# Second tile's h loads on ScalarE's queue, weight staging re-spaced, first units reordered

## What is computed

```python
# layer 0: MLP whose last 128 outputs come from an expert picked by an index
h = gelu(einsum('bnd,hd->bnh', x, fc1_w) + fc1_b)              # hidden 2048
y = concat([einsum('bnh,sh->bns', h, fc2_w) + fc2_b,           # 384 outputs
            einsum('bnh,bph->bnp', h, experts_w[indices]) + experts_b[indices][:, None, :]], -1)
x = x + y
# layer 1: a linear layer picked by an index
x = x + einsum('bnh,boh->bno', x, weight[subject_id]) + bias[subject_id][:, None, :]
# layer 2: causal averages over time, gates, a normalised output
ctx = causal_ema(x, tau_ctx)
wg = sigmoid(einsum('btc,ec->bte', concat([x, ctx], -1), Wg) + bg)
# ... four gated traces, their blend "temporal" ...
gate = sigmoid(einsum('btc,ec->bte', temporal, Wtemp) + btemp)
soma = gelu(einsum('btc,ec->bte', x, Wsoma) + bsoma)
x = x + layernorm(einsum('btc,ec->bte', soma * gate, Wout)) * gamma + beta
# layer 3: a linear layer picked by an index
x = x + einsum('bnh,boh->bno', x, weight[ids]) + bias[ids][:, None, :]
```

## Time and profile before

| | before |
|---|---|
| median of 2 runs | 1416.73 us (1415.06 to 1418.4) |
| profiled execution | 1426.79 us, span 1425.1 us |
| PE busy | 1342.4 us, 94% of the span, 5725 matmuls |
| VectorE (DVE) busy | 1059.9 us, 74% |
| ScalarE (ACT) busy | 673.9 us, 47% |
| mean granted TensorE clock | 0.974 |
| DMA | 196.57 MB, mean 138 GB/s |

### The profile page before, as it was taken

One profiled execution on the slowest core, in us unless ns is written; L12 is line 12 of the kernel. 1 busy time (PEld: TensorE's weight loads), 2 busy tenths in 40 slices (PEclk: granted clock), 3 DMA queues, 4 the chain that ended last, 5 costly groups with the idle time before them and its releaser, 6 DMA issues.

```text
span 1425.1 us, 16400 instructions
## 1 busy us (share of the span) xinstructions
PE 1342.4 (94%) x5725; PEld 1090.7 (77%) x5725; DVE 1059.9 (74%) x1643; ACT 673.9 (47%) x1237; POOL 102.3 (7%) x135
## 2 busy tenths in 40 slices
PE   8889897989998999899999998999999999999998
PEld 6667685767786878787788787787888888888887
...
GB/s 259 77 93 200 196 152 81 130 184 169 197 137 137 111 206 204 187 133 134 141 228 236 208 157 175 178 185 51 104 45 163 52 97 54 153 71 54 99 8 67
DMA packets 102123, 196.57 MB, mean 138 GB/s; under 512 B 9705, under 2 KB 28137, under 8 KB 98969
## 3 DMA queue, kind: packets, MB, share of 16 engines
...
...
## 4 chain that ended last, share of the span: by engine, by line
PE 68%; DVE 16%; DMA 6%; ACT 5%; issue 4%; SPq 0%; DVEq 0%; POOL 0%; ACTq 0%; POOLq 0%
PE bank L1413 23%; PE bank L1414 22%; PE bank L1415 22%; DMA hb_in<-hb_dram 3%; DVE drive L2079 2%; DVE x_hl L1844 2%; DVE w_hl L1844 1%; DVE h_hl L1844 1%; DVE drive L2066 1%; DVE temporal L2094 1%; DMA stage<-in_wg 1%; ACT h_hl L983 1%; ACT bank L979 1%; DVE hb_out L1938 1%; DVE t_lo L1844 1%
## 5 line engine op out<-in xcount | busy, mean ns | idle before, releaser
L1413 PE MATMUL bank<-t_hi,sp_hl 128*128 128x512 f32 x448 | 186.6, 416 | 56.4 <-ACT p_sb L963 33.9
L1413 PE MATMUL bank<-h_hl,w_hl 128*128 128x512 f32 x512 | 203.4, 397 | 20.4 <-DVE w_hl L1844 20.2
L1415 PE MATMUL bank<-h_hl,w_hl 128*128 128x512 f32 x512 | 202.1, 395 | 0.0
L1414 PE MATMUL bank<-h_hl,w_hl 128*128 128x512 f32 x512 | 201.8, 394 | 0.0
L1414 PE MATMUL bank<-t_lo,sp_hl 128*128 128x512 f32 x448 | 182.7, 408 | 0.0
L1415 PE MATMUL bank<-t_hi,sp_hl 128*128 128x512 f32 x448 | 182.1, 406 | 0.0
L1413 PEld LDWEIGHTS bank<-t_hi,sp_hl 128*128 128x128 f32 x448 | 89.2, 199 | 86.1 <-ACT p_sb L963 39.4
L1413 PEld LDWEIGHTS bank<-h_hl,w_hl 128*128 128x128 f32 x512 | 97.9, 191 | 45.2 <-DVE h_hl L1844 24.8
L1415 PEld LDWEIGHTS bank<-h_hl,w_hl 128*128 128x128 f32 x512 | 97.6, 191 | 20.9
L1414 PEld LDWEIGHTS bank<-h_hl,w_hl 128*128 128x128 f32 x512 | 97.9, 191 | 20.2
L1415 PEld LDWEIGHTS bank<-t_hi,sp_hl 128*128 128x128 f32 x448 | 88.9, 199 | 19.7
...
## 6 DMA issues: line engine op xcount, KB each, us to landing
...
hb_dram<-hb_out SPq DMA_DIRECT2D x64, 256.0 KB, 3.7
hb_in<-hb_dram SPq DMA_DIRECT2D x64, 256.0 KB, 3.4
...
stage<-in_l_w SPq DMA_DIRECT2D x32, 256.0 KB, 3.4
...
```

The lines of the kernel that those rows point to most:

```text
L1413: eng.matmul(ps, w_hi, x_hi, start=first, stop=False, skip_group_check=resumed)
L1414: eng.matmul(ps, w_hi, x_lo, start=False, stop=False, skip_group_check=resumed)
L1415: return eng.matmul(ps, w_lo, x_hi, start=False, stop=final, skip_group_check=resumed)
```

## The change

The change has four parts. (1) `load_hb` moves from SP's list to ScalarE's: block 0's load stands ahead of the second tile's first split, block j + 1's at the head of block j's work. On SP the second tile holds only the staging and the expert weights' loads; in the last pair the loads of x, gate weights and soma weights, which stood between the h loads, follow each other. C12's store, and C12's Gelu on ScalarE, move behind P1's copy of the next unit; C12's addition on VectorE moves ahead of C21's low part. (2) Staging: two tables now say in which unit or block the parts are staged (pair 0 at j = 2, 6, 9, 12, pairs 1 and 2 at 3, 7, 11; unit 0 of pairs 1 to 3 now has one), TE parts all come before the WG parts, and of two parts in a unit the first one is split in mid-unit, the other at the end. (3) The first units of pair 0 run P6 before P5 (but for k = 0), and ScalarE's and VectorE's lists for them are in another order. (4) The loads of x's parts T3/B22 stand ahead of the reads of the indices, and seven of the eight reads come later.

```diff
-        FIRST_ORDER = ("P5", "P6", "P4", "P7", "P3")
+        FIRST_ORDER = [("P5", "P6", "P4", "P7", "P3")] + 3 * [("P6", "P5", "P4", "P7", "P3")]
...
-        PARKED = [("N1", 0)] + [("SO", c) for c in range(KC)] + [("TE", c) for c in range(2)]
-        PARKED += [("WG", c) for c in range(2 * KC)] + [("TE", c) for c in range(2, KC)]
+        PARKED = [("N1", 0)] + [("SO", c) for c in range(KC)] + [("TE", c) for c in range(KC)]
+        PARKED += [("WG", c) for c in range(2 * KC)]
...
+        parked_units = ((4, 5, 6, 7, K8 + 2, K8 + 6, K8 + 9, K8 + 12),
+                        (0, 1, 2, 4, 5, 7, K8 + 3, K8 + 7, K8 + 11),
+                        (0, 1, 2, 3, 4, 5, 6, 7, K8 + 3, K8 + 7, K8 + 11),
+                        (0, 1, 1, 2, 3, 4, 5, 6, 7))
+        l1_units = ((4, 5, 6, 7), (2, 3, 5, 6), (2, 3, 4, 5), (2, 3, 4, 5))
...
             load_w2(0)
+            load_part_b(0, 0)
+            load_part_b(0, 1)
             on.wait_ge(s_idx, 32)
-            expert = [nc.sync.value_load(idx[0:1, b:b + 1], min_val=0, max_val=EXPERTS - 1) for b in range(B)]
-            subject = [nc.sync.value_load(idx[0:1, B + b:B + b + 1], min_val=0, max_val=SUBJECTS - 1)
-                       for b in range(B)]
+            expert = [nc.sync.value_load(idx[0:1, 0:1], min_val=0, max_val=EXPERTS - 1)]
...
             for p in range(PAIRS):
                 for k in range(K8):
+                    if k:
+                        store_hb(p, k - 1, 0)
...
-                    store_hb(p, k, 0)
-                load_hb(p, 0)
+                if p < PAIRS - 1:
+                    load_part_b(p + 1, 1)
+                store_hb(p, K8 - 1, 0)
                 pass_staged(p, K8 - 1)
-                if p == PAIRS - 1:
-                    break
-                load_part_b(p + 1, 1)
-                for j in range(1, HC):
-                    load_hb(p, j)
+                for j in range(HC if p < PAIRS - 1 else 0):
                     if j in (10, 13):
+                        on.wait_ge(s_fc2, 2 * HC * p + HC + j - 3)
                         load_exp(p + 1, int(j == 13))
-                    if j >= 3:
-                        pass_staged(p, K8 + j - 3)
-                for j in range(HC - 3, HC):
                     pass_staged(p, K8 + j)
 
-            for j in range(1, HC):
-                load_hb(PAIRS - 1, j)
-                if j == 2:
-                    load_xt(0)
-                if j in (3, 5, 7):
-                    load_wg((j - 1) // 2)
...
+            load_xt(0)
+            load_wg(1)
+            load_wg(2)
+            load_wg(3)
+            load_wsoma(2)
+            load_wsoma(3)
+            store_x2(LAST - 1)
+            load_wsoma(0)
+            load_wsoma(1)
```

On ScalarE, in a unit:

```diff
                 p1_of(p, k)
+                if k:
+                    h_of_c12(p, k - 1)
...
                 h_of_c22(p, k)
-                for n in ahead[6:7]:
-                    product_hi(n)
+                staged_hi(p, k, slice(0, -1))
...
-                h_of_c12(p, k)
...
-                staged_hi(p, k)
+                staged_hi(p, k, slice(-1, None))
```

On ScalarE, behind a pair's units and in its second tile:

```diff
+                h_of_c12(p, K8 - 1)
+                load_hb(p, 0)
                 w2_hi(2 * HC * p + HC - 1)
                 for j in range(HC):
+                    if j + 1 < HC:
+                        load_hb(p, j + 1)
                     hb_hi(v)
```

On VectorE, in a unit:

```diff
                     product_lo(n)
+                staged_lo(p, k, slice(0, -1))
                 if p and k == 0:
-                    x1_of(t, 0)
-                    x1_of(t, 1)
+                    for m in range(KC):
+                        x1_of(t, m)
+                c12_of(p, k)
                 for n in ahead[6:7]:
                     product_lo(n)
...
-                h_lo_c21(p, k)
-                if p and k == 0:
                     x1_lo(t, 0)
                     x1_lo(t, 1)
-                c12_of(p, k)
+                h_lo_c21(p, k)
...
-                staged_lo(p, k)
+                staged_lo(p, k, slice(-1, None))
```

More of the change, by code:

```diff
@@ L1218, in _, with staged_hi @@
                 h_of_c21(0, k)
[L1219 to L1222 removed]
+            def staged_hi(p, u, at=slice(None)):
+                for n in staged_in[p, u][at]:
                     kind, a = staging[n]
@@ L1256, in unit @@
                     x1_hi(t, 1)
+                for n in ahead[6:7]:
+                    product_hi(n)
                 h_of_c21(p, k)
```

90 lines of the change are left out of this document (39 added, 51 removed).

## The result

The changed kernel takes 1355.78 us (median of two, 1355.22 to 1356.33) against 1416.73, a ratio of 0.957, 95% interval 0.9518 to 0.9621: 61 us faster. The profiled execution spans 1354.6 us where that of before spans 1425.1, 70.5 us less. The kernel before varies: beside the later experiments it took 1415 to 1435 us, and its profiled execution, 1426.8, is longer than the two timed here. The changed kernel's two times agree within 1 us.

A forecast was written before the change was run, and what follows sets the result against it. First 880 us bound by 116 us of PE waiting and half clock, the rest by PE. Stage gains summed to 83.0 us, off the profiled 1426.8 giving 1343.8, stated as 1340 because of slow stores; range 1322 to 1368.

The forecast's parts named there:

- The forecast case: Whole kernel: the stage gains come as summed, about 1340 us, own range 1322 to 1358; chance 0.70.
- sum of 83.0: First 880 us: gains of all nine stages added, 83.0 us, taken off the profiled 1426.8 to give 1343.8.
- the two stalls for P6: Unit 1 of pairs 2 and 3: new stalls of about 5 and 4 us, released by P1's copy.
- the last stall of about 6 us: Near the end of the last second tile: one stall of about 6 us, from a late h load, stays.
- (1 - clock) x us: First 880 us: clock loss reckoned per stage as missing clock share times stage time, 38 us in all.
- the 37.0: Pair 1's first tile, 214 to 378 us: gain of 37.0 from 23.4 idle and 14.8 of clock lost, about 1.2 left.
- paid twice: PE stalls over 2.3 us: half-clock matmuls follow as well, counted as 1.7 us for a stall of 2.3 to 6.
- Left 0.3: Second tile of pair 0, 154 to 214 us: of 8.0 us lost only 0.3 stays, gain 7.7.
- a limit of 6.5 us: Second tiles: an h load landing within about 6.5 us is hidden by issuing one block ahead; median landing 3.4.
- the first rival: Second tiles: h loads gain nothing from their new queue, landing above 6.5 us whenever stores run; 1362 us, chance 0.13.
- the staging rival: Unit 0 of pairs 1 to 3: staging stalls move instead of going, growing to about 8 us; 1366 us, chance 0.10.
- ScalarE's own waits: Second tiles, rival: ScalarE's order couples h loads to its waits, slower; up to 1580 us, chance 0.03.

The follow-up runs named there:

- e5: Changed kernel, but POOL stores the first tile's x lows of pairs 0 to 2 in units 0 and 1 of the next pair; 1376.5 us.
- e9: Changed kernel with POOL's x stores spaced, one every two fc2 blocks, and one a block in the last pair; 1342.2 us.
- e1: Changed kernel with the h loads put back on SP's queue, weight loads of the last second tile spaced between them again; 1386.3 us.
- e2: Kernel before with only the h loads moved to ScalarE's queue, one block ahead; 1410.1 us.
- e3: Changed kernel with the old staging of parts (all at the unit's end); 1386.8 us.
- e4: Kernel before with the new staging tables alone, h loads on SP and orders as before; 1409.1 us.
- e8: Changed kernel with the first four units' order as before, early loads of the x parts kept; 1371.9 us.

## Why the prediction was right, and where it was off

The forecast was 1340 with 1322 to 1368, faster; it is 1355.8. The forecast case came true in most of its mechanisms: SP's waits ahead of the h loads, the gate parts' shared buffers and the new part in unit 0, each shown by a run or a chain above. The sum of 83.0 was 12.5 too large against the profile's 70.5. It would have been further off without luck: the stages that fell short did so by 19 us together, and 4.5 us in the last second tile and 2.0 in units 4 to 7 came unforecast.

Of the signs that were named, the two stalls for P6 (5 and 4 forecast, 4.82 and 3.71 measured), the x parts' loads at 5.97 us and the free gate parts came. Not so the last stall of about 6 us, and the first second tile is not free of stalls. And one sign of being wrong came: h loads that land in over 6.5 us in the first three pairs, 11.7, 11.4 and 10.1 us at most. So the view of the second tiles was wrong in that point, although the time fell into the range. Point by point:

**The clock was mis-sized, the largest error.** I took (1 - clock) x us for each stage and added it to PE's idle time. The clock is low in the idle time too, where it costs nothing. Stretches of 4 us of the kernel before around its stall at 291.90:

```profile
284.00:288.00 4.00, 0.00 (x0) 0.00 (x0) 0.00 (x0) 0.00 (x0) 0.00 (x0) 0.66 0.92 196
288.00:292.00 4.00, 0.10 (x1) 0.10 (x1) 1.53 (x3) 1.42 (x3) 0.00 (x0) 0.50 0.04 14
292.00:296.00 4.00, 4.00 (x11) 3.13 (x12) 2.90 (x8) 2.14 (x5) 0.00 (x0) 0.56 0.48 168
```

By my rule these are 1.4 + 2.0 + 1.8 = 5.1 us; 8 matmuls at half clock make 1.6. For pair 1's first tile I had 14.8, and its 40 matmuls cost 8.0: the 37.0 becomes 30, and 30.5 was gained. In all, 131 x 0.20 = 26 us were there, not 38. Nor does every stall over 2.3 us bring a half clock, as the prediction's "paid twice" has it: behind the 2.95 us at 387.16 in after there is none.

**Second tiles.** "Left 0.3" for pair 0 was wrong: 2.34 us of stall and 7 half-clock matmuls stayed, gain 4.0 for 7.7. I held a landing against a limit of 6.5 us by its median of 3.4; but four x stores start in blocks 10 to 13 of the sixteen, and the chain of after shows what they do to the load of block 15:

```profile
373.70 11.45 DMA hb_in<-hb_dram
```

This also put 2.95 and 1.64 us on the first product of pairs 2 and 3, where I had nothing. Pair 2's first tile gained 3.8 us for 10.0: 2.95 of the gap are this stall, and 2.1 the clock, 27 matmuls or 5.4 us where I had 7.5. It is the first rival, in part: it had named landings above 6.5 us whenever stores run. e5 and e9 show that POOL's stores are the cause: with the stores behind the second tile the landings in the first three pairs are 4.7 us at most, with the stores spaced 7.3.

**Unit 0's staged part.** 5.0, 3.8 and 1.2 us forecast; 4.82, 3.71 and 1.11 measured. In after's timelines of VectorE and ScalarE the chain is the one that was added up (402.53 is the last step of the output part, then its split, a product split, the copy for which PE waited until 404.52):

```profile
402.53 0.49 DVE L1972 TENSOR_SCALAR stage<-stage,wout_mean 128x512 f32<-128x512 f32 x1
```

```profile
403.05 0.63 ACT L907 ACTIVATE stage_hi<-stage 128x512 fp32r<-128x512 f32 x1 [3.60 <-DVE stage L1972]
403.59 0.40 ACT L927 ACTIVATE sp_hl<-fc_raw 128x256 fp32r<-128x256 f32 x1
403.89 0.58 ACT L951 ACTIVATE p_sb<-bank 128x512 f32<-128x512 f32 x1
```

**Gate parts and order.** The distances of a unit or four blocks were enough; neither the staging rival nor ScalarE's own waits came about: an issue takes ScalarE 0.33 us, and it waits 73.7 us for h where it waited 70.8 before, off the path. I had thought of the parts of the change as a sum of stages. e1 to e4 show them as conditions of each other, though the stage sums, which were of all parts together, were not spoiled by it.

**Head.** 11.8 for 12.7: the 3.3 us of stalls left in unit 0 are 1.12 and 2.20 us. The part that I gave to the early loads is not shown: alone, in the old order, they bring nothing (e8), and the new order was not run with the loads at their old time. Units 4 to 7 gave 6.5 for 4.5: 4.6 of it is idle time, 62.1 - 60.3 = 1.8 is PE's busy time for the same products. In part that is the first matmul behind each of the short waits that are gone, behind which the next starts after 0.33 or 0.34 us and not after 0.23; the rest stays open.

**The last stall** I kept at 5.79 us, with 17.28 of landing. It went, 4.5 us: 1.36, 1.00 and 0.77 us are there now. e1 puts 1.68 and 4.42 us back, so it was SP's order in part and not the DMA engines alone.

**The 10 us between profile and median** probably lay in what was removed (70.5 by the profiles, 61 by the medians; from 880 us on both kernels take 545 us), so 1343.8 was the better figure to correct than 1334. No trace of a short execution of the kernel before is there to show it.
